# First cross attention of a decoder: the turn of the maxima placed ahead of the second round of scores

## What is computed

```
q = (x1 @ Wq + bq).reshape(Bn, Nq, H, D).transpose(0, 2, 1, 3)      # 16 heads of 8
k = x2 @ Wk + bk ; v = x2 @ Wv + bv
k = jnp.concatenate([k, memory_k], axis=1)                          # 128 + 120 keys
v = jnp.concatenate([v, memory_v], axis=1)
attn = softmax(jnp.einsum('bhqd,bhkd->bhqk', q, k) * scale)
out = jnp.einsum('bhqk,bhkd->bhqd', attn, v)
x = layernorm(x + out @ Wp + bp)
```

## Time and profile before

| what | value |
|---|---|
| time, median of 3 runs | 3201.68 us (3196.98 to 3204.82) |
| the profiled execution | 3206.08 us, of which 3204.3 us is the span from the first to the last instruction |
| the stage of the first cross attention | about 724 to 1420 us of the span |
| TensorE busy over the span | 2850.8 us (89%) |
| VectorE, ScalarE, GpSimd busy | 2216.2, 1785.0, 1511.7 us |

### The profile page before, as it was taken

How to read it: one execution, slowest core, us unless ns; L and a number is a source line. 1 busy time by engine, 2 the same in 40 slices (tenths; PEclk the granted TensorE clock), 3 DMA queues, 4 the chain that set the end, 5 groups by cost and what they waited for, 6 DMA issues and landing times. The chain is left out here.

```text
span 3204.3 us, 88723 instructions
## 1 busy us (share of the span) xinstructions
PE 2850.8 (89%) x26256; PEld 2336.8 (73%) x26383; DVE 2216.2 (69%) x6122; ACT 1785.0 (56%) x6327; POOL 1511.7 (47%) x3745
## 2 busy tenths in 40 slices
PE   2499999979999999978888969999999899999995
PEld 2388888866666666648667758888888688888884
DVE  1277777756666666656333459999998488888887
ACT  1265556644555555531456647777777466666663
POOL 0144444442333333317675458777777244444442
PEclk7799999988999999989999989999999899999997
DMA  9200000001111111103332211111110100000000
GB/s 220 26 23 22 22 22 23 23 26 32 38 38 37 37 36 36 32 24 89 80 78 72 64 49 44 41 44 42 41 44 27 29 27 26 26 23 26 26 20 11
DMA packets 244002, 131.80 MB, mean 41 GB/s; under 512 B 47904, under 2 KB 237728, under 8 KB 243872
## 3 DMA queue, kind: packets, MB, share of 16 engines
q1 hardware_dynamic: 235168, 112.22, 13.9%
q0 software_dynamic: 8704, 17.97, 1.7%
HBM read 73.34 MB, written 48.51 MB: 38 GB/s over the span
## 5 line engine op out<-in xcount | busy, mean ns | idle before, releaser
L1096 ACT ACTIVATE pr<-psS,small 128x128 f32<-128x128 f32 x1024 | 364.9, 386 | 183.9 <-DVE small L1186 166.7
L1503 ACT ACTIVATE pr<-psT 120x512 f32<-120x512 f32 (+1 forms) x512 | 278.0, 595 | 279.2 <-PE psT L1409 279.2
L835 POOL TENSOR_SCALAR pr<-pr,small 128x128 f32<-128x128 f32 (+1 forms) x1024 | 359.6, 373 | 34.5 <-DVE small L778 28.3
L1249 POOL TENSOR_SCALAR self_Qx<-self_qk,headmask 128x128 f32<-128x128 f32 x1024 | 370.3, 387 | 0.0
L1548 DVE TENSOR_REDUCE small<-psS 128x4 f32<-128x992 f32 x256 | 303.3, 1185 | 92.5 <-PE psS L1413 92.3
L1399 PE MATMUL psT<-cross_Qm,cross_xf 32*120 32x512 f32 (+1 forms) x1024 | 307.2, 643 | 33.8 <-DVE cross_xoT L1596 30.4
L847 POOL TENSOR_TENSOR small<-small,eps 128x1 f32<-128x1 f32 x128 | 24.5, 191 | 659.5 <-issue 382.5
L615 ACT ACTIVATE pr<-psS,small 128x120 f32<-128x120 f32 x512 | 185.9, 392 | 172.2 <-DVE small L797 172.2
L1058 PEld LDWEIGHTS psS<-self_qk,self_Qx 128*128 128x128 f32 x2048 | 254.8, 192 | 18.6 <-issue 0.3
L1058 PE MATMUL psS<-self_qk,self_Qx 128*128 128x128 f32 x2048 | 257.0, 276 | 0.0
L1096 ACT ACTIVATION_READ_ACCUMULATOR pr<-psS,small 128x1 f32 x1024 | 228.9, 224 | 0.0
(11 more groups left out here) (337 smaller groups left out, 8344.3 us busy)
## 6 DMA issues: line engine op xcount, KB each, us to landing
self_parts<-results SPq DMA_DIRECT2D x64, 192.0 KB, 2.3
experts_xb<-slots SPq DMA_DIRECT2D x144, 65.0 KB, 1.9
slots<-zeros SPq DMA_DIRECT2D x72, 128.0 KB, 5.8
between<-self_xo SPq DMA_DIRECT2D x128, 64.0 KB, 1.6
cross_x<-between SPq DMA_DIRECT2D x128, 64.0 KB, 1.8
cross_res<-between SPq DMA_DIRECT2D x128, 64.0 KB, 1.7
cross_cx<-in_ctx SPq DMA_DIRECT2D x128, 60.0 KB, 1.8
self_x<-in_x SPq DMA_DIRECT2D x64, 64.0 KB, 1.7
```

Of the source, the lines that this page charges most:

```text
L835: last = pool.tensor_scalar(pr[w.slot][:, h * P:h * P + keys], pr[w.slot][:, h * P:h * P + keys], inv[w.slot][:, h:h + 1], 1.0, ALU.mult, ...
L1096: last = act.activation(pr[e.slot % 4][:, cols], K.S[e.slot % 2][:, cols], ACT.Exp, bias=nmax[e.slot % 4][:, n:n + 1], accum_out=tot[k.slo ...
L1249: last = pool.tensor_scalar(Qx[b.slot % 2][:, h, :], qk[b.slot][:, 0:P], K.headmask[:, h:h + 1], 1.0, ALU.mult, ALU.mult)
L1503: act.activation(PT[k][0:sizes[ck], half], T[0:sizes[ck], half], ACT.Exp).then_inc(exped, 1)
```

## The change

On TensorE the turn of the maxima (with its wait for the maxima of round 0 and for the split) moves from behind `scores(c, 1)` to ahead of it, right behind the first `weigh`. The waits for the later work on the turned output stay behind `scores(c, 1)`. On VectorE the cast moves ahead of the wait for `bn_stats`. No instruction is added or dropped.

```diff
                 def step(c):
                     a, m, n, o = c + 2, c - 1, c - 3, c - 2
+                    z, v = c - 5, c - 6
                     scores(c, 0)
                     weigh(c - 2, 0)
-                    scores(c, 1)
-                    z, v = c - 5, c - 6
-                    if z.live:
-                        need(pe, normed, z.done())
-                        need(pe, turned_sb, v.done())
                     if m.live or z.live:
                         need(pe, maxed, c.done(R, 1) if c.live else nseq * R)
                     if m.live:
...
                             last = pe.matmul(S[0][:, P * j:P * j + P], diag[m.slot % 2][:, P * j:P * j + P], K.identb[:],
                                              start=True, stop=True)
                         last.then_inc(nb_ps, 1)
+                    scores(c, 1)
+                    if z.live:
+                        need(pe, normed, z.done())
+                        need(pe, turned_sb, v.done())
                     if not z.live and v.live:
                         need(pe, turned_sb, v.done())
...
-                    if w.live:
-                        need(dve, counted, w.done())
                     if m.live:
                         need(dve, nb_ps, m.done())
                         dve.tensor_copy(NB[m.slot % 2][:], S[0][:, 0:512]).then_inc(nb_sb, 1)
+                    if w.live:
+                        need(dve, counted, w.done())
```

## The result

The changed kernel takes 3230.57 us (median of 6 runs, 3227.45 to 3232.16) against 3203.25 us for the kernel before beside it (6 runs, 3196.98 to 3209.19). The ratio is 1.0083 [1.0070, 1.0097], or +27.3 us. The forecast was 3215.5 us in a range of 3200 to 3231, so the direction and the range held; the forecast size, +14 us, was half of the measured one.

What follows compares the result with a forecast made beforehand. TensorE was taken to bound the kernel, a shift of round 2 shifting the step. Held turn +0.27, open waits +0.19, copy -0.19 gave +0.27 us per step, +14 us over 52 steps: 3215.5 us, range 3200 to 3231.

Steps and rivals of the forecast that it cites:

- What bounds the kernel: TensorE, busy 278.2 of 300 us, sets the 10.61 us step; a shift of round 2 shifts the whole step.
- The held turn: On TensorE the turn now waits for the maxima of round 0, formerly covered by round 1: +0.27 us per step.
- Round 1 behind the turn: On TensorE, register work of round 1's waits, no longer hidden by a backlog, adds 0.19 us per step.
- The second part: A wait between the two first matmuls of round 1 on TensorE, no longer hidden, costs another 0.10 us.
- The copy: On VectorE, `xoT` no longer queues behind the cast and ends earlier: -0.19 us per step.
- the last step's 0.78: Time from the start of line 1457 to the end of `xoT` with no cast in the way; 0.97 in the loop.
- the other end: Lower bound of the copy's gain: nothing, if the loop's address work for the logits costs as much as the cast.
- VectorE's order: Moving VectorE's wait for `bn_stats` behind the cast was claimed to be free, as its consumer comes later.
- B, the draw: TensorE's waits run beside the turn's matmuls, or its answer to the maxima is shorter: 3199 to 3211 us, chance 0.28.
- C, the turn that finds its maxima ready: The turn meets no hold and the copy's gain is pure: -10 to -15 us, 3190 us, chance 0.06.
- D: More TensorE idling drops the granted clock at times; ten slow steps would be +38 us, giving 3253 us; chance 0.06.
- The other sign of failure: Prediction is wrong if round 2 waits for the exponentials of line 1503 instead of the copy; margin 0.1 to 0.2 us.

Runs made afterwards that it cites:

- split_before: Kernel before, with round 2's wait for the copy `xoT` moved from ahead of the round to its second half: 3187.63 us, ratio 0.9948.
- t_first_before: Kernel before with round 2's copy wait at its second half, VectorE's part of the change, and round 2's psT matmuls ahead of the cast wait: 3172.96 us.
- early_max: Changed kernel with the maxima of round 0 moved ahead of VectorE's sum for the layer norm: 3222.94 us, ratio 1.0064.
- waits_first: Changed kernel with round 1's three waits (cast, maxima, exponentials) placed ahead of the held turn: 3229.61 us, ratio 1.0075.
- small_full: Kernel before with one added 8-column matmul over all 128 rows, and a long-met wait, between `weigh` and round 1: 3213.23 us, ratio 1.0029.
- copyfirst_after: Changed kernel with VectorE's copy `xoT` ahead of the copy of the logits, the signal on the later of the two: 3225.00 us, ratio 1.0060.
- dve_only: Kernel before with only VectorE's part of the change, its wait for `bn_stats` behind the cast: 3202.06 us, ratio 0.9993.
- split_after: Changed kernel with round 2's wait for the copy `xoT` moved to ahead of its second half: 3210.97 us, ratio 1.0022.
- pe_only: Changed kernel with VectorE's list as before, so TensorE's part of the change alone: 3224.32 us, ratio 1.0069.

## Why the prediction was right, and where it was too small

**What bounds the kernel.** Right. TensorE's list is what the step follows. `split_before` and `t_first_before` shorten the step by shortening TensorE's waits, and a shift of round 2 is a shift of the whole step.

**The held turn, +0.27 forecast, +0.338 measured.** The mechanism is right: the wait appears on the turn with the maxima's name, and in `early_max` it shrinks by as much as the maxima come earlier. The step that was mis-sized is the answer. I took the shortest one in the trace, 0.06, for TensorE's answer to the maxima; it is 0.13 in the loop (1.349 - 1.218). In the written-out step shown above it is 0.06: its maxima, in VectorE's timeline below, end at 797.98, and the turn starts at 798.04.

```profile
796.80 1.18 DVE L1548 TENSOR_REDUCE small<-psS 128x4 f32<-128x992 f32 x1
```

**Round 1 behind the turn, +0.19 forecast, +0.091 measured.** The 0.33 between turn and round 1 came out as stated and for another reason, so that this number agrees is luck. The failed step is the price of these waits, "So 0.11 for each, 0.33 for three": `waits_first` took all three away from there and the gap stayed. What stands in its place is the switch from whole-array matmuls to tiles, 0.11 in `small_full`. The row that the price was read from stands: the first two matmuls of round 2 are 0.115 apart in the loop and 0.01 in the written-out steps. What failed is carrying it over to round 1. The second part, a stagger of 0.10 between the two first matmuls of round 1, is not there at all (0.01). The 50 to 100 ns for each read that the Trainium skill gives (Advanced Engine Details and Errata, Miscellaneous Facts, Network/Comms), by the estimate 0.15 to 0.30 for the three, do not show here either: round 1 follows the turn by 0.325 with them in between and by 0.324 without (`waits_first`).

**What I had not on the list: +0.048 at the gate.** Line 1457 follows the gate by 0.244 instead of 0.196, in the new place of the gate behind tiled matmuls. My sum has no term for it.

**The copy, -0.19 forecast, -0.091 measured.** The direction is right. The failed step is the choice of the last step's 0.78 for the loop. I had named the other end, that the loop's address work for the logits costs as much as the cast did, and took the measured row; the truth lay between. `copyfirst_after` gives the 0.78 once the first operation has no such address.

**VectorE's order, "free", 0.064 measured.** Wrong, and two thirds of the 0.10 that was missing at the copy are this.

**The sum.** By the forecast's terms: 0.338 (0.27) + 0.091 and 0 (0.19) + 0.046 (0) - 0.091 (-0.19) = +0.384 (+0.27). The terms for the waits and for the copy were both too large by 0.10 and of opposite sign, so their errors cancelled; what is left of the error is the answer in the hold (0.07) and the gate (0.05). It is luck that two wrong sizes left the total inside the range, whose upper end is 0.4 us above the measured median. The difference of 0.114 times 52 is 6 us. Of the other 7 us that were missing on the median, 3.1 lie at the two ends of the stage, where I had given about nothing: 1.0 between the written-out casts, and 2.1 ahead of the first cast and behind the last, most of it because the cast has another place in its step. 1.6 is the scatter ahead of the stage, and the last 2.6 lie between the profiled execution (+24.7) and the medians (+27.3).

**The rivals.** B, the draw, needed the turn's waits to run beside its matmuls. They do, and yet the gap stays, since it isn't made of waits; and the hold alone is 0.338. C, the turn that finds its maxima ready, fails by the row of waits. D fails by the clock of 1.00. Its price of a step, 14.38 us, I called partly the filling of the pipeline; `dve_only` does the same step in 9.65 at the upper clock, so the filling was no part of it. The other sign of failure that I gave, round 2 waiting for the exponentials, seems to be there by name in 46 brackets, but round 2 follows the copy by 0.236 as before, and `copyfirst_after` and `split_after` show the exponentials with time to spare.

## What to carry to other kernels

Before moving an operation ahead of another, ask what its wait was covered by: a wait that costs nothing behind 1.3 us of work cost 0.34 us a step without it. Put a wait at the first instruction that needs it; moving two waits by some instructions, with the two matmuls that then could go first, gave 1%, more than the reorder lost. On TensorE, count the changes between whole-array and tiled matmuls along the list and keep the kinds together, since the 0.1 us of each shows as busy time and in no view of waits.

## What the runs showed of the hardware that I had not expected

- One whole-array matmul of 8 columns between tiled ones costs 0.11 us; the same over 32 rows costs nothing measurable (0.003 us per step).
- VectorE's answer to TensorE was, in the means, 0.04 us for the cast of `dve_only` and 0.12 for the copy of `copyfirst_after`, both with a fixed address, and 0.16 us for the logits of `pe_only`, whose address is worked out in the loop, or 0.22 with a long-met wait just ahead of them, though the engine had been idle for over 1 us.
- The first step between casts took 14.4 us at a granted clock of 0.50 to 0.66 and 9.65 us at 1.00, with the same list on TensorE (the kernel before and `dve_only`); the kernel before and the changed one both had the slow one.
- TensorE's answer to VectorE ranged from 0.06 to 0.24 us within one program: 0.13 for the maxima in the loop and 0.06 in the written-out step, 0.24 for the copy or the cast ahead of round 2.
- Three long-met waits in TensorE's list between the held turn and round 1 cost nothing (0.325 us with them, 0.324 without).
